# A four-layer graph network on one core: order of TensorE's first work, and transfers of 125 rows issued in two parts

## The chip, the cores and the metric

The kernel runs on one core of a Trainium2 chip. The metric is device time in microseconds (us) of one execution; the median of several runs is quoted, and the profile is of one execution more. The engines are TensorE (PE; its weight loads are shown as PEld), VectorE (DVE), ScalarE (ACT), GpSimd (POOL) and SyncE (SP), which only issues transfers. Each engine runs its own program, and programs meet through semaphores.

## The reference

The input is a graph with N = 1250 nodes of D = 512 features and E = 21250 edges, sorted by receiver `dst` (10000 random pairs in both directions, and 1250 loops). Four layers follow one another, and each is added to its input and normalised over the features:

```python
edge_index = jnp.stack([src, dst])
x = _layernorm(x + L0(x))   # graph attention, 8 heads; batch norm, gelu, plus x @ W_skip + b_skip
x = _layernorm(x + L1(x))   # messages weighted by an MLP of the edges' 8 features, times 4 edge attributes
x = _layernorm(x + L2(x))   # attention over neighbours, then silu(agg) @ base_w.T + cubic splines of agg
x = _layernorm(x + L3(x))   # relu(w @ [x, mean of the neighbours])
```

For L0, with `h = x @ W_gat` in 8 heads, the score of an edge is `leaky(a_src[src] + a_dst[dst])`, a softmax over the edges of each receiver weights `h[src]`, and a sum by receiver follows. L1 gathers `x0, x1 = x @ W_up` at each edge's sender, multiplies by `tpw = MLP(edge_attr_8)` and `edge_attr_4`, and sums by receiver. L2's attention is of the same kind with one head.

## The kernel before, in words

Nodes are cut into NB = 10 blocks of NP = 125 rows, so that most tiles have 125 partitions, and edges into 125 lists of 170.

**First stage.** SP loads dst, src, two tiles of edge attributes and the blocks 5 to 9 of x (L539 to L543), then 16 small attention vectors (L549), clears `recs`, a table of edge records in DRAM (L554), and loads weights. ACT loads the blocks 0 to 4 of x (L1420) and W_gat (L1421). VectorE makes 40 masks of dst and scans them (L1852), whose totals `tot_e` go to TensorE (L814, L815: block totals, "record order"). From their result VectorE (L1866 on) finds each record's position, and POOL scatters the 170 lists of records to `recs` (L717). A second set of masks and a scan (L1908) give totals for the order of the count tiles; TensorE's count_order (L819, L820) answers to them. Then 17 sort rounds follow, each with VectorE (L1949 to L1952), ACT's scale_lanes (L1456) and TensorE's sort_batch (L828).

TensorE's order before is written out by hand: block totals; transposes of x in ten blocks (x_block, L838); gat blocks 0 to 4 (`x @ W_gat`, L845); count_order; w_transposed (transposes of W_gat, L866); attention products (L884); gat blocks 5 to 7; two small products (L891, L892); the sort, with gat blocks 8 and 9 in rounds 3 and 8. ACT copies the results out in the same order (gat_out, L1461).

**The stage's end.** When the scatter is done, ACT loads records back in lanes (L1543) and TensorE transposes them (L1000) for L1's MLP (products to L1025). VectorE's max stage (L2037) and the MLP stand ahead of the attention heads, whose first step is row_products (L1030).

**Later transfers.** L1 stores its blocks `xup` (ACT's copy L1663, SP's store), and POOL gathers from them by edge. L2 makes tiles in VectorE (L2067, L2071) for products with x on TensorE (L1261, L1290); deg, a row sum of all counts, is one reduction (L2314) after the last tile; then the sums are divided (L2319 to L2325), weight_sums (L2331 to L2334, 12 operations) and node_sums (L2344 to L2347) feed the spline products (L1309, L1319). L3 splits `z` in a high and a low part, stores both to `z_rows` (ACT the high parts, SP the low), and POOL gathers some rows of it (big_z, read at L1400 by TensorE). Last, SP stores ten blocks of the output (L672).

Of the kernel before, what the change touches and what calls it, by code (L numbers as in the profile page):

```python
# [7 lines left out]
N, D, E = 1250, 512, 21250  # L8
H, C = 8, 64
# [84 lines left out]
def build(nc, a, out):  # L94
# [8 lines left out]
    with ctx:  # L103
# [328 lines left out]
        s_w0_in = sem("s_w0_in")  # L432
        s_wl2_in = sem("s_wl2_in")
# [97 lines left out]

        def bass_row(v, p):
            return v.rearrange("(a n) -> a n", a=1).to_broadcast([p, v.shape[0]])
# [3 lines left out]
        def _(sp):  # L537

            sp.dma_start(dsti, a["dst"].rearrange("(p e) -> p e", p=NP)).then_inc(s_dst_in, 16)  # L539
            sp.dma_start(srci, a["src"].rearrange("(p e) -> p e", p=NP)).then_inc(s_rec_in, 16)  # L540
            sp.dma_start(a4, a["edge_attr_4"].rearrange("(p e) k -> p e k", p=NP)).then_inc(s_rec_in, 16)
            sp.dma_start(a8, a["edge_attr_8"].rearrange("(p e) k -> p e k", p=NP)).then_inc(s_rec_in, 16)
            sp.dma_start(x_sb[:, HB:, :], a["x"].rearrange("(b p) n -> p b n", p=NP)[:, HB:, :]).then_inc(s_x_in1, 16)  # L543
# [97 lines left out]
            sp.dma_start(cnt_rows.rearrange("(b p) n -> p b n", p=NP), cnt_s[:]).then_inc(s_cntrow_out, 16)  # L641
# [24 lines left out]
            for b in range(NB):  # L666
                sp.wait_ge(s_zlo_ok, b + 1)
                sp.dma_start(z_rows[N + b * NP:N + (b + 1) * NP, :], z_lo[:NP, b, :].bitcast(f32)).then_inc(s_zrow_out, 16)
# [8 lines left out]
        def _(pool):  # L677
# [86 lines left out]
            def gathers(i, par, tiles):  # L764
                pool.wait_ge(s_gld_in0 if par == 0 else s_gld_in1, i * 16 + 16)
                pool.nop(nofuse=True)
                g3 = gld[:, par, :]
                pool.wait_ge(s_sel_ok, i * (2 * TP) + (TP * par + TP))
                pool.nop(nofuse=True)
                pool.tensor_copy(gidx[:, par, :], g3.bitcast(u32).rearrange("p (t k) -> p t k", k=RW)[:, :, R_SRCI])  # L770
                pool.tensor_copy(gslot[:, par, :], g3).then_inc(s_gidx_ok, 1)
                pool.wait_ge(s_gidx_ok, i * 2 + (par + 1))
                if par == 0:
                    pool.wait_ge(s_xup_out0, 16 * NB // 2)
                    pool.wait_ge(s_xup_out1, 16 * NB // 2)
# [16 lines left out]
            pool.wait_ge(s_cntrow_out, 16)  # L792
# [3 lines left out]
            pool.wait_ge(s_zrow_out, 16 * 2 * NB)  # L796
# [6 lines left out]
        def _(pe):  # L803
# [28 lines left out]
            def x_block(b):  # L832
                if b % HB == 0:
                    pe.wait_ge(s_x_in if b == 0 else s_x_in1, 16)
# [582 lines left out]
        def _(act):  # L1417
            A = nc.scalar.activation

            act.dma_start(x_sb[:, 0:HB, :], a["x"].rearrange("(b p) n -> p b n", p=NP)[:, 0:HB, :]).then_inc(s_x_in, 16)  # L1420
            act.dma_start(w_gat, kview(a["L0_gnn_W_gat"])).then_inc(s_w0_in, 16)  # L1421
# [49 lines left out]
            for b in range(HB):  # L1471
                gat_out(b)
            for c in range(KT):
                w_transposed(c)
            act.wait_ge(s_wt_ps, KT + 1)
# [3 lines left out]
            for b in range(HB, NB - 2):  # L1479
                gat_out(b)  # L1480
# [11 lines left out]
            for j in range(ROUNDS):  # L1492
                scale_lanes(j)
                if j in (4, 9):
                    gat_out(NB - 2 + j // 9)
# [163 lines left out]
            def xup_out(b):  # L1659
                act.wait_ge(s_xup_ps, b + 1)  # L1660
                if b >= 2:
                    act.wait_ge(s_xup_out0 if b % 2 == 0 else s_xup_out1, 16 * (b // 2))
# [137 lines left out]
            def store_high(b):  # L1800
                act.wait_ge(s_z_cp, b + 1)
                act.dma_start(z_rows[b * NP:(b + 1) * NP, :], z_hi[:NP, b, :].bitcast(f32)).then_inc(s_zrow_out, 16)
# [32 lines left out]
        def _(dve):  # L1835
# [9 lines left out]
            dve.wait_ge(s_dst_in, 16)  # L1845
# [11 lines left out]
            dve.wait_ge(s_rec_in, 48)  # L1857
# [443 lines left out]
            def half_step(u, hf):  # L2301
# [12 lines left out]
            link(v.tensor_reduce(deg[:], cd, X, ALU.add))  # L2314
# [3 lines left out]
            dve.wait_ge(s_l2_agg, 3)  # L2318
            ins = v.tensor_scalar(rden2, PS[:, 0:3, :].rearrange("p a n -> p (a n)")[:, 0:N], 0.5, None, ALU.max)  # L2319
            ins.then_inc(s_psum_ok, 1)  # L2320
            dve.wait_ge(s_psum_ok, NB)
            link(v.reciprocal(rden2, rden2))
            for f in range(KT - 1):
                dve.wait_ge(s_l2_cp, f + KT)
                v.tensor_tensor(aggT[:, f, :], aggT[:, f, :], rden2, ALU.mult).then_inc(s_aggT_ok, 1)  # L2325
# [9 lines left out]

            def node_sums(g):
# [56 lines left out]
            for g in range(3):  # L2393
                weight_sums(g)
# [130 lines left out]
```

## Time and profile before

| what | us |
|---|---|
| median of 3 runs (lowest, highest) | 1581.47 (1580.15, 1582.06) |
| the profiled execution, its own time | 1582.99 |
| its span in the profile | 1581.48 |
| TensorE busy | 1373.6 (87%) |
| VectorE busy | 1354.2 (86%) |
| ScalarE busy | 903.0 (57%) |
| GpSimd busy | 480.1 (30%) |

The span is the time from the first instruction to the last in the profile; what lies outside it (1.5 us) is start and end. By the page's chain of work that ended last, 51% of the span is TensorE's, 24% VectorE's, 12% issue time, and 5% each ACT's and the transfers'. Rows of a timeline give the start, the duration, the engine and line, output and inputs with shapes, how many, and in brackets how long the engine had been idle and what ended that.

### The profile page before, as it was taken

What the parts mean: (1) busy time and instruction counts of PE and PEld (TensorE: products, weight loads), DVE (VectorE), ACT (ScalarE), POOL (GpSimd) and SP (SyncE); (2) the same over time, 40 slices, a digit from 0 to 9 for tenths busy, and PEclk for the clock granted to TensorE, in tenths of its full rate; (3) what the DMA queues carried; (4) which work ended last, traced back from release to release, by engine and by line L of the source; (5) the groups of instructions that cost most, each with busy time, mean ns of one, the idle gap of its engine ahead of it and who ended that gap; (6) DMA issues with size and microseconds to landing.
All of it is one profiled execution on the core that took longest, in us unless ns stands there. A gap on an engine that the chain in (4) does not pass through costs nothing.

```text
span 1581.5 us, 25111 instructions
## 1 busy us (share of the span) xinstructions
PE 1373.6 (87%) x8237; PEld 885.5 (56%) x8237; DVE 1354.2 (86%) x2065; ACT 903.0 (57%) x1949; POOL 480.1 (30%) x488
## 2 busy tenths in 40 slices
PE   1978898837688887789999999979999999999997
PEld 1555444602333333566666666756667777776465
DVE  8875999899899999759999999777989979996244
ACT  1286555628565565558888888543168849772300
POOL 1788888840000100236666666200000000000000
PEclk9998999859899999689999999989999999999998
DMA  4201000126111210246666766400144444342301
GB/s 128 69 6 9 6 7 7 14 70 192 53 58 48 60 52 17 77 133 212 198 201 193 214 197 196 76 1 1 54 132 135 134 145 170 136 143 69 117 24 43
DMA packets 76686, 150.26 MB, mean 95 GB/s; under 512 B 13722, under 2 KB 32268, under 8 KB 76477
## 3 DMA queue, kind: packets, MB, share of 16 engines
q1 hardware_dynamic: 50531, 83.18, 16.1%
q0 software_dynamic: 23328, 59.50, 15.0%
q10 hardware_dynamic: 2746, 6.59, 1.3%
q8 instruction: 38, 0.62, 0.2%
q14 instruction: 43, 0.35, 0.1%
HBM read 116.13 MB, written 32.91 MB: 94 GB/s over the span
## 4 chain that ended last, share of the span: by engine, by line
PE 51%; DVE 24%; issue 12%; ACT 5%; DMA 5%; DVEq 2%; POOL 0%; SPq 0%; POOLq 0%; ACTq 0%
PE PS L1309 14%; DVE arena L2071 7%; DVE arena L2037 5%; PE PS L1167 5%; PE PS L1261 4%; PE PS L1319 4%; DVE arena L2067 3%; PE PS L931 3%; PE PS L1394 3%; PE PS L1153 3%; DVE arena L2233 3%; ACT arena L1456 2%; PE PS L845 2%; DMA x_sb<-in_x 2%; PE PS L1374 2%
## 5 line engine op out<-in xcount | busy, mean ns | idle before, releaser
L717 POOL DMA_INDIRECT recs<-arena x170 | 239.3, 1408 | 89.4 <-issue 88.8
L1079 PE MATMUL PS<-arena 125*128 125x512 f32 (+1 forms) x480 | 190.1, 533 | 43.4 <-DVE arena L2071 43.3
L781 POOL DMA_INDIRECT arena<-xup,gidx x205 | 194.8, 950 | 104.7 <-issue 52.4
L1167 PEld LDWEIGHTS PS<-arena 128*32 128x32 f32 x3280 | 174.1, 109 | 88.3 <-ACT arena L1694 81.9
L1694 ACT ACTIVATE arena<-arena,gslot 128x32 f32<-128x32 f32 x820 | 186.3, 309 | 55.2 <-PE PS L1167 48.0
L1167 PE MATMUL PS<-arena 128*32 128x128 f32 (+1 forms) x3280 | 201.9, 306 | 6.2 <-DVE arena L2225 3.9
L2225 DVE TENSOR_TENSOR arena<-PS,arena 128x1536 f32<-128x1536 f32 (+1 forms) x103 | 179.0, 1738 | 0.0
L1079 PEld LDWEIGHTS PS<-arena 125*128 125x128 f32 x480 | 85.6, 191 | 147.8 <-issue 77.6
L1626 ACT ACTIVATE arena<-arena,c 125x1250 f32<-125x1250 f32 x80 | 106.7, 1336 | 97.6 <-DVE arena L2067 97.6
L2067 DVE SCALAR_TENSOR_TENSOR arena<-arena,c 125x1250 f32<-125x1250 f32 (+1 forms) x100 | 137.7, 1380 | 14.0 <-ACT arena L1748 12.9
L1309 PE MATMUL PS<-arena,cnt_d 128*125 128x256 f32 x576 | 148.4, 380 | 0.0
L794 POOL DMA_INDIRECT cnt_d<-cnt_rows,bidx_c x1 | 0.9, 946 | 463.8 <-DVE bvalid L2453 463.8
L1309 PE MATMUL PS<-arena 128*125 128x256 f32 x432 | 118.1, 383 | 3.6 <-DVE cnt_d L2347 3.5
L1309 PEld LDWEIGHTS PS<-arena,cnt_d 128*125 128x125 f32 x576 | 108.7, 189 | 16.4
L1153 PE MATMUL PS<-arena 64*128 64x512 f32 x410 | 117.5, 649 | 0.0
L2071 DVE SCALAR_TENSOR_TENSOR arena<-arena,cnt_s 125x1250 f32<-125x1250 f32 x80 | 116.0, 1450 | 0.0
L1512 ACT ACTIVATE arena<-PS 125x626 uint16<-125x626 f32 x102 | 69.2, 692 | 60.1 <-PE PS L931 60.0
L1309 PEld LDWEIGHTS PS<-arena 128*125 128x125 f32 x432 | 81.6, 189 | 30.7 <-issue 20.2
L2221 DVE TENSOR_TENSOR arena<-PS,arena 128x512 f32<-128x512 f32 (+1 forms) x103 | 70.9, 688 | 19.4 <-DMA arena<-xup,gidx 14.8
L931 PE MATMUL PS<-arena 128*125 128x512 bf16 (+1 forms) x408 | 73.1, 311 | 15.8 <-DVE arena L1992 15.4
L2233 DVE TENSOR_TENSOR arena<-PS,arena 128x256 f32 x205 | 84.8, 414 | 1.3 <-PE PS L1167 0.5
L931 PEld LDWEIGHTS PS<-arena 128*125 128x125 bf16 x408 | 44.6, 142 | 63.7 <-DVE arena L1992 38.9
(395 smaller groups left out, 2536.2 us busy)
## 6 DMA issues: line engine op xcount, KB each, us to landing
arena<-in_spline_wT SPq DMA_DIRECT2D x32, 512.0 KB, 4.1
t_rows<-arena SPq DMA_DIRECT2D x18, 512.0 KB, 5.1
arena<-t_rows SPq DMA_DIRECT2D x18, 512.0 KB, 4.5
arena<-uv_rows SPq DMA_DIRECT2D x14, 610.4 KB
arena<-h_rows SPq DMA_DIRECT2D x26, 256.0 KB
h_rows<-arena SPq DMA_DIRECT2D x24, 256.0 KB, 2.8
arena<-xup,gidx POOLq DMA_INDIRECT x205, 3.7
cnt_rows<-cnt_s SPq DMA_DIRECT2D x1, 3051.8 KB
```

The lines of the kernel that those rows point to most:

```text
L717: pool.indirect_dma_start(out=recs, out_offset=bass.IndirectOffsetOnAxis(pos[:, c:c + 1], 0), in_=rec[:, c, :], in_offset=None).then_inc(s ...
L781: pool.indirect_dma_start(out=ring[:, m, :], out_offset=None, in_=xup, in_offset=bass.IndirectOffsetOnAxis(gidx[:, par, m:m + 1], 0))\
L931: ins = t.matmul(PS[:NP, 2 * (n % 3) + q, 0:n1 - n0], oh_dst[:, n % (2 * WP), :, e], oh_src[:, 2 * (n % WP) + e, n0:n1], start=(e == 0), s ...
L1079: ins = t.matmul(PS[:, 3 * par + q, 0:n1 - n0], hs[:, sblk, par * C:par * C + 2 * C], wt[:, sblk % WR, n0:n1], start=(sblk == 0), stop=(sb ...
L1153: t.matmul(PS[:, tpw_bank[(2 * k + q) % 4], :], h3[r, buf, k * 128:(k + 1) * 128], w_m4[r, :], start=True, stop=True, tile_position=(q * H ...
L1167: ins = t.matmul(PS[quad * DB:(quad + 1) * DB, bank, o0 * MUL:o0 * MUL + w], sel4[:, s, v * DB:(v + 1) * DB], prod[:, s, c0 * MUL:c1 * MUL ...
L1309: ins = t.matmul(PS[:NP, bank, c * HD:(c + 1) * HD], lhs, w_part(g, w), start=(s == 0 and m in ((0, 1, 3, 6) if j == 0 else (0, 1, 3))), s ...
L1694: ins = A(sel4[:, s, y * DB:(y + 1) * DB], eq4[:, m // 4, s * DB:(s + 1) * DB], ACT.Copy, scale=gslot[:, par, c + R_Y + y:c + R_Y + y + 1])
L2067: v.scalar_tensor_tensor(dst, U, cc, V, ALU.add, ALU.max).then_inc(ok, 1)
L2071: v.scalar_tensor_tensor(dst, e, 1.0, cm, ALU.min, ALU.mult).then_inc(ok, 1)
L2225: v.tensor_tensor(pr[:, :, :, 1:4, :], w[:, :, :, 1, :].unsqueeze(3).to_broadcast([128, n, 2, 3, MUL]), xg[:, :, 1:4, :].unsqueeze(2).to_b ...
L2233: v.tensor_tensor(d, PS[:, 2 + m % 4, 0:256], d, ALU.add).then_inc(s_gsum_ok, 1)
```

## The change

There are three edits. (1) Every transfer of 125 rows becomes two, one of 112 rows and one of 13, with the counts of the waits doubled: the loads of dst, src, edge attributes and x, the stores of xup, of the count rows, of z (SP's and ACT's) and of the output. (2) TensorE's order in the first stage is x blocks, w_transposed, gat 0 and 1, block totals, attention products, gat 2 to 8, count_order, gat 9, small products, sort (without gat blocks). ACT copies in the same order. W_gat's load has a semaphore of its own. (3) At the spline's start, the reduction for deg is done in two halves, the first ahead of the tiles of half 0 and the second in the old place; the first three weight_sums stand ahead of the wait for TensorE's sums; the products of the aggregate are made in the order 0, 2, 1, and the first silu waits for two of them instead of three.

```diff
+        ROWS = (slice(0, NP // 16 * 16), slice(NP // 16 * 16, NP))
...
-            sp.dma_start(dsti, a["dst"].rearrange("(p e) -> p e", p=NP)).then_inc(s_dst_in, 16)
-            sp.dma_start(srci, a["src"].rearrange("(p e) -> p e", p=NP)).then_inc(s_rec_in, 16)
...
-            sp.dma_start(x_sb[:, HB:, :], a["x"].rearrange("(b p) n -> p b n", p=NP)[:, HB:, :]).then_inc(s_x_in1, 16)
+            for dst_tile, view, done in (
...
+                    (x_sb[:, HB:, :], x_rows[:, HB:, :], s_x_in1)):
+                for r in ROWS:
+                    sp.dma_start(dst_tile[r], view[r]).then_inc(done, 16)
...
-                sp.dma_start(xup[b * NP:(b + 1) * NP, :], xup_st[:, b % 2, :]).then_inc(s_xup_out0 if b % 2 == 0 else s_xup_out1, 16)
+                for r in ROWS:
+                    sp.dma_start(xup[b * NP:(b + 1) * NP, :][r], xup_st[r, b % 2, :])\
+                      .then_inc(s_xup_out0 if b % 2 == 0 else s_xup_out1, 16)
...
-                sp.dma_start(out[b * NP:(b + 1) * NP, :], x_sb[:, b, :]).then_inc(s_out_done, 16)
-            sp.wait_ge(s_out_done, 16 * NB)
+                for r in ROWS:
+                    sp.dma_start(out[b * NP:(b + 1) * NP, :][r], x_sb[r, b, :]).then_inc(s_out_done, 16)
+            sp.wait_ge(s_out_done, 32 * NB)
...
-            pe.wait_ge(s_tot_ok, 1)
-            t.matmul(PS[:NP, 1, 0:NDB], upper[:NP, :NP], tot_e[:], start=True, stop=True)
-            t.matmul(PS[:, 1, 64:64 + NDB], ones[:NP, 0:128], tot_e[:], start=True, stop=True).then_inc(s_order_ps, 1)
+            def record_order():
+                pe.wait_ge(s_tot_ok, 1)
...
             for b in range(NB):
                 x_block(b)
-            pe.wait_ge(s_w0_in, 16 * (1 + 2 * H))
-            for b in range(HB):
-                gat_block(b)
-            count_order()
+            pe.wait_ge(s_wgat_in, 16)
             for c in range(KT):
                 w_transposed(c)
+            for b in range(2):
+                gat_block(b)
+            record_order()
+            pe.wait_ge(s_w0_in, 16 * 2 * H)
             pe.wait_ge(s_wa_cp, KT)
...
-            gat_block(HB)
-            for b in range(HB + 1, NB - 2):
+            for b in range(2, NB - 1):
                 gat_block(b)
+            count_order()
+            gat_block(NB - 1)
...
             for j in range(ROUNDS):
                 sort_batch(j)
-                if j in (3, 8):
-                    gat_block(NB - 2 + j // 8)
...
-                    act.wait_ge(s_aggT_ok, KT + 1 if h else KT - 1 + s)
+                    act.wait_ge(s_aggT_ok, KT + 1 if h else KT if s else KT - 2)
...
+            def degrees(hf):
+                bs = slice(hf * HB, (hf + 1) * HB)
+                link(v.tensor_reduce(deg[:, bs], cd[:, bs, :], X, ALU.add))
+            degrees(0)
             half_tiles(0)
             half_terms(1)
             half_tiles(1)
             for j in range(1, NB):
                 add_tile(j)
-            link(v.tensor_reduce(deg[:], cd, X, ALU.add))
+            degrees(1)
...
+            for g in range(3):
+                weight_sums(g)
+
+            dve.wait_ge(s_l2_agg, 3)
...
+            for f in (0, 2, 1):
+                dve.wait_ge(s_l2_cp, f + KT)
+                v.tensor_tensor(aggT[:, f, :], aggT[:, f, :], rden2, ALU.mult).then_inc(s_aggT_ok, 1)
...
-            for g in range(3):
-                weight_sums(g)
             node_sums(0)
```

## Rows read from the trace of the kernel before

**Rows 1.** Chain of waits: start, duration in us, and what.
```profile
2.60 35.35 DMA x_sb<-in_x
...
689.29 4.10 DMA xup<-arena
...
1159.81 7.97 PE PS L1309 x28
...
1169.49 6.04 PE PS L1309 x28
...
1484.25 14.90 DMA z_rows<-z_lo
...
1504.53 6.21 PE PS L1394 x20
...
1514.41 4.67 PE PS L1394 x20
```

**Rows 2.** Windows: length; busy of five engines; granted clock, DMA share, GB/s.
```profile
8.50:12.50 4.00, 0.00 (x0) 0.00 (x0) 3.97 (x35) 0.08 (x1) 0.00 (x0) 1.00 0.92 246
15.00:20.00 5.00, 0.00 (x0) 0.00 (x0) 5.00 (x1) 0.00 (x0) 0.00 (x0) 1.00 0.32 130
400.00:407.00 7.00, 5.38 (x29) 4.65 (x30) 1.64 (x6) 4.06 (x9) 0.63 (x1) 0.60 0.13 37
658.00:661.00 3.00, 1.97 (x8) 1.45 (x7) 2.85 (x6) 2.98 (x4) 0.00 (x0) 0.50 1.05 373
1450.00:1480.00 30.00, 28.35 (x91) 14.10 (x90) 9.81 (x28) 15.53 (x22) 0.95 (x1) 1.00 0.29 98
1576.00:1580.00 4.00, 0.00 (x0) 0.00 (x0) 0.00 (x0) 0.00 (x0) 0.00 (x0) 0.50 0.31 104
```

**Rows 3.** Timeline of the first stage.
```profile
27.14 0.61 PE L814 MATMUL PS<-tot_e,upper 125*125 125x40 f32 x2 [27.14 <-DVE tot_e L1855]
...
28.97 0.20 DVE L1866 TENSOR_SCALAR ngi_e<-PS 128x40 int32<-128x40 f32 x1
...
38.00 4.64 PE L838 MATMUL PS<-ident,x_sb 125*128 125x125 f32 x20 [5.40 <-DMA x_sb<-in_x]
...
42.43 18.03 PE L845 MATMUL PS<-arena 128*125 128x512 f32 x40
...
45.67 1.38 POOL L717 DMA_INDIRECT recs<-arena  x1 [37.88 <-issue]
...
61.99 1.14 PE L866 MATMUL PS<-ident,arena 128*128 128x128 f32 x8 [0.25 <-ACT arena L1465]
...
63.82 3.75 PE L884 MATMUL PS<-arena 128*128 128x16 f32 x32 [0.69 <-ACT arena L1465]
...
80.18 14.75 ACT L1456 ACTIVATE arena<-arena 125x128 f16<-125x128 f16 x50
...
97.64 0.60 ACT L1461 ACTIVATE arena<-PS 125x512 f32<-125x512 f32 x1 [2.71 <-PE PS L845]
```

**Rows 4.** Timeline of the first stage's end.
```profile
337.88 0.35 ACTq L1543 DMA_DIRECT2D arena<-recs  x1
...
342.60 1.09 PE L1000 MATMUL PS<-ident,arena 128*128 128x128 f32 x4 [24.24 <-DVE mxh L2039]
...
400.72 4.56 PE L1030 MATMUL PS<-ident,uv 125*125 125x125 f32 x20 [8.54 <-DVEq L2057]
```

**Rows 5.** Timeline of the later stages.
```profile
688.67 0.60 ACT L1663 ACTIVATE arena<-PS 125x512 f32<-125x512 f32 x1 [1.91 <-DMA xup<-arena]
...
1062.29 1.65 DVE L2067 SCALAR_TENSOR_TENSOR arena<-arena,c 125x625 f32<-125x625 f32 x2 [2.87 <-ACT arena L1748]
...
1125.11 13.17 DVE L2314 TENSOR_REDUCE deg<-cnt_d 125x10 f32<-125x12500 uint16 x1
...
1159.81 1.88 PE L1309 MATMUL PS<-arena 128*125 128x256 f32 x4 [3.48 <-DVE cnt_d L2347]
...
1504.07 0.47 PE L1400 MATMUL PS<-big_z,big_cnt 128*125 128x512 f32 x1 [2.84 <-ACT big_z L1829]
```

More of the change, by code:

```diff
@@ L537, in _ @@
         def _(sp):
-            sp.dma_start(dsti, a["dst"].rearrange("(p e) -> p e", p=NP)).then_inc(s_dst_in, 16)
-            sp.dma_start(srci, a["src"].rearrange("(p e) -> p e", p=NP)).then_inc(s_rec_in, 16)
-            sp.dma_start(a4, a["edge_attr_4"].rearrange("(p e) k -> p e k", p=NP)).then_inc(s_rec_in, 16)
-            sp.dma_start(a8, a["edge_attr_8"].rearrange("(p e) k -> p e k", p=NP)).then_inc(s_rec_in, 16)
-            sp.dma_start(x_sb[:, HB:, :], a["x"].rearrange("(b p) n -> p b n", p=NP)[:, HB:, :]).then_inc(s_x_in1, 16)
+            x_rows = a["x"].rearrange("(b p) n -> p b n", p=NP)
+            for dst_tile, view, done in (
+                    (dsti, a["dst"].rearrange("(p e) -> p e", p=NP), s_dst_in),
+                    (srci, a["src"].rearrange("(p e) -> p e", p=NP), s_rec_in),
+                    (a4, a["edge_attr_4"].rearrange("(p e) k -> p e k", p=NP), s_rec_in),
+                    (a8, a["edge_attr_8"].rearrange("(p e) k -> p e k", p=NP), s_rec_in),
+                    (x_sb[:, HB:, :], x_rows[:, HB:, :], s_x_in1)):
+                for r in ROWS:
+                    sp.dma_start(dst_tile[r], view[r]).then_inc(done, 16)
             sp.wait_ge(s_wdiag_zero, 1)
@@ L640, in _ @@
             sp.wait_ge(s_psum_ok, NB)
-            sp.dma_start(cnt_rows.rearrange("(b p) n -> p b n", p=NP), cnt_s[:]).then_inc(s_cntrow_out, 16)
+            for r in ROWS:
+                sp.dma_start(cnt_rows.rearrange("(b p) n -> p b n", p=NP)[r], cnt_s[r]).then_inc(s_cntrow_out, 16)
             for g in range(2 * SUBS):
@@ L667, in _ @@
                 sp.wait_ge(s_zlo_ok, b + 1)
-                sp.dma_start(z_rows[N + b * NP:N + (b + 1) * NP, :], z_lo[:NP, b, :].bitcast(f32)).then_inc(s_zrow_out, 16)
+                for r in ROWS:
+                    sp.dma_start(z_rows[N + b * NP:N + (b + 1) * NP, :][r], z_lo[r, b, :].bitcast(f32)).then_inc(s_zrow_out, 16)
             for b in range(NB):
                 sp.wait_ge(s_x_ok, 3 * NB + b + 1)
-                sp.dma_start(out[b * NP:(b + 1) * NP, :], x_sb[:, b, :]).then_inc(s_out_done, 16)
-            sp.wait_ge(s_out_done, 16 * NB)
+                for r in ROWS:
+                    sp.dma_start(out[b * NP:(b + 1) * NP, :][r], x_sb[r, b, :]).then_inc(s_out_done, 16)
+            sp.wait_ge(s_out_done, 32 * NB)
         @block.gpsimd
@@ L811, in _ @@
             pe.wait_ge(s_consts, 1)
-            pe.wait_ge(s_tot_ok, 1)
-            t.matmul(PS[:NP, 1, 0:NDB], upper[:NP, :NP], tot_e[:], start=True, stop=True)
-            t.matmul(PS[:, 1, 64:64 + NDB], ones[:NP, 0:128], tot_e[:], start=True, stop=True).then_inc(s_order_ps, 1)
+            def record_order():
+                pe.wait_ge(s_tot_ok, 1)
+                t.matmul(PS[:NP, 1, 0:NDB], upper[:NP, :NP], tot_e[:], start=True, stop=True)
+                t.matmul(PS[:, 1, 64:64 + NDB], ones[:NP, 0:128], tot_e[:], start=True, stop=True).then_inc(s_order_ps, 1)
             def count_order():
@@ L1418, in _ @@
             A = nc.scalar.activation
-            act.dma_start(x_sb[:, 0:HB, :], a["x"].rearrange("(b p) n -> p b n", p=NP)[:, 0:HB, :]).then_inc(s_x_in, 16)
-            act.dma_start(w_gat, kview(a["L0_gnn_W_gat"])).then_inc(s_w0_in, 16)
+            for r in ROWS:
+                act.dma_start(x_sb[r, 0:HB, :], a["x"].rearrange("(b p) n -> p b n", p=NP)[r, 0:HB, :]).then_inc(s_x_in, 16)
+            act.dma_start(w_gat, kview(a["L0_gnn_W_gat"])).then_inc(s_wgat_in, 16)
             def ln_sqrt(layer, b):
@@ L1470, in _ @@
                   PS[:, 4 + b % 2, :].rearrange("p (k n) -> p k n", k=KT)[:, :, 0:NP], ACT.Copy).then_inc(s_xt_cp, 1)
-            for b in range(HB):
-                gat_out(b)
             for c in range(KT):
                 w_transposed(c)
+            for b in range(2):
+                gat_out(b)
             act.wait_ge(s_wt_ps, KT + 1)
@@ L1477, in _ @@
             A(wa[:, :, 0:2 * H], PS[:, 2, 0:KT * 2 * H].rearrange("p (k n) -> p k n", k=KT), ACT.Copy).then_inc(s_wa_cp, 1)
-            for b in range(HB, NB - 2):
+            for b in range(2, NB):
                 gat_out(b)
@@ L1801, in store_high @@
                 act.wait_ge(s_z_cp, b + 1)
-                act.dma_start(z_rows[b * NP:(b + 1) * NP, :], z_hi[:NP, b, :].bitcast(f32)).then_inc(s_zrow_out, 16)
+                for r in ROWS:
+                    act.dma_start(z_rows[b * NP:(b + 1) * NP, :][r], z_hi[r, b, :].bitcast(f32)).then_inc(s_zrow_out, 16)
             def x3_in(b):
@@ L2313, in _ @@
                 add_tile(j)
-            link(v.tensor_reduce(deg[:], cd, X, ALU.add))
+            degrees(1)
             link(v.tensor_scalar(cen[:], cen[:], -KAPPA, KAPPA * (1.0 + 1.0 / STEP), ALU.mult, ALU.add))
[L2318 to L2325, printed above, removed]
             def weight_sums(g):
@@ L2334, in weight_sums @@
                 v.tensor_tensor(t4, b21, t2w, ALU.subtract)
+            for g in range(3):
+                weight_sums(g)
+            dve.wait_ge(s_l2_agg, 3)
+            ins = v.tensor_scalar(rden2, PS[:, 0:3, :].rearrange("p a n -> p (a n)")[:, 0:N], 0.5, None, ALU.max)
+            ins.then_inc(s_psum_ok, 1)
+            dve.wait_ge(s_psum_ok, NB)
+            link(v.reciprocal(rden2, rden2))
+            for f in (0, 2, 1):
+                dve.wait_ge(s_l2_cp, f + KT)
+                v.tensor_tensor(aggT[:, f, :], aggT[:, f, :], rden2, ALU.mult).then_inc(s_aggT_ok, 1)
             def node_sums(g):
```

19 lines of the change are left out of this document (9 added, 10 removed).

## The prediction

> **What bounds the kernel now.** I read the chain of waits first: it names the work that ended last, and an edit off it gains nothing by itself. Seven of its rows carry this forecast [rows 1]. It begins with one transfer, the second half of x, from 2.60 for 35.35 us, and goes on in TensorE's work on x. Later it runs through the stores of blocks and their read-back: 4.10 us for an xup store, 14.90 us for the last z store.
>
> The windows by stretch say why these are long [rows 2]. While only transfers of 125 rows run (15 to 20, and 1576 to 1580) the DMA share is 0.32 and 0.31, at 130 and 104 GB/s: five engines in sixteen are at work. From 8.5 to 12.5, where W_gat (128 rows) runs beside x, the share is 0.92 at 246 GB/s; with 128-row loads alone, from 658, it is 1.05 at 373 GB/s.
>
> Third I read the timelines. In the first stage [rows 3] TensorE waits at L814 for the totals (27.14) and at L838 for x's second half (38.00). At the stage's end [rows 4] the attention heads start at 400.72, behind 8.54 us of waiting on VectorE's max stage. The MLP ahead of them started only at 342.60, when the scattered records came back from the load at 337.88. So two chains lead to the heads: the sort and max stage on VectorE, and scatter, record load and MLP.
>
> **Term 1, first stage: −6.0 us.** The start loads 2 × 1.28 MB of x, 1.05 MB of W_gat, 0.085 MB each of dst and src and 1.02 MB of edge attributes: 4.8 MB. With all parts on sixteen engines at the 373 GB/s of the 128-row row, that is 12.9 us; from a first byte at about 2.0 and with 1.3 us to land, the second half of x is there at about 16.3 (22.8 at the 246 GB/s of the mixed row) instead of 37.95. Both rates are bounds from rows; parts of 112 and 13 rows appear in neither, and I take the faster, since its transfers are alone, as these would be.
>
> TensorE then does its blocks 5 to 9 (4.64 us, L838), w_transposed (two groups like L866's, 2.5 us with the wait between; up to 3.9 cold) and two gat blocks. L845's five blocks took 18.03, so 3.6 us each; I allow 7.8 for two, with a cold start. The new wait for W_gat stands ahead of all this; its load is shared out with x's and should be in by 16 too, and while it isn't, everything on TensorE is held. The block totals, which before ran at 27.14, come at 16.3 + 4.6 + 3.9 + 7.8 = 32.6 and end at 33.1. VectorE's next step, L1866, goes from 28.97 to 33.2: **4.2 us late**. This is the cost of the new order: totals wait behind work that is not urgent. The 4.2 us goes rigidly into the record positions and POOL's scatter (first at 45.67), which is 170 issues long and doesn't depend on the sort. The records' load thus comes at 342.1 instead of 337.88. Before, L1000 began 4.7 us after that issue and last waited for VectorE's mxh, so the load was in earlier, by something between 0 and 2 us; with 0.7 the MLP is 3.5 us late.
>
> SP's queue: the attention loads (L549), the clearing of recs and the loads after them stand behind x's second half and come about 20 us earlier; the products (L884, 3.75 us) wait for them at 33.2, behind the totals, and they should be in by some 27. If they weren't, gat blocks 2 to 8 and count_order would wait too. The count order itself comes at 33.1 + 3.75 + 7 × 3.6 + 0.5 = 62.6, against 42.43 + 18.03 = 60.5 before: 2 us later, with 19.7 us between it and the sort's start on ACT at 80.18.
>
> The sort gains. Its start at 80.18 follows gat_out of block 7, and inside it two gat blocks cost ACT 2.71 us of waiting and 0.60 of work each [rows 3]: 2 × 3.31 = 6.6 us. Blocks 8 and 9 now lie before it; TensorE is through with block 9 by 67, so that the start, which followed block 7 at 80, is VectorE's to set and may move up by 1 or 2. So 6.6 to 8.6; I take 8.3, and VectorE reaches the heads at 392.3. The MLP is the later one: its last product before the heads came 8.54 us ahead of 400.72, at 392.2, plus 3.5 = 395.7. The heads gain 400.7 − 395.7 = 5.0.
>
> The clock: from 400 to 407 the granted clock is 0.60, after TensorE has idled through those 8.54 us, and L1030's 20 transposes take 4.56 us. With no idle ahead of them at full clock they would take as little as half; between 0 and 2.3 I take 1.0. Sum: −6.0.
>
> **Term 2, xup stores: −3.3.** Two stores follow one another on the chain, the last 4.10 us; ACT's L1663 waits 1.91 us for the first of the two [rows 5]. A store is 256 KB, so 2.3 us at some 111 GB/s (the rows give 98 to 130 [rows 2]) and 1.75 us of fixed time. At 373 GB/s the bytes take 0.7: −1.6 and −1.7. Lower bound nothing, if the second part's issue (about 0.3 us on SP) and landing cost what the bytes save.
>
> **Term 3, spline start: −1.6.** The degree reduction L2314 is 13.17 us, after VectorE's last tile [rows 5]. Half of it, 6.6, now stands before the tiles, where VectorE had 2.87 us of idle (L2067 at 1062.29). The other 3.7 to 3.8 us delays the tiles and the aggregation behind them. TensorE ends that at 1156.3 + 3.8 = 1160.1 and finds its input made, where before it idled 3.48 us (L1309): VectorE has saved the other half of the reduction, and the weight sums no longer stand in line. So +3.8 − 3.48. The first spline group behind the idle took 7.97 us, the next 6.04 [rows 1]; without the idle, −1.93. Together −1.6. Bounds: +0.3 if the clock gives nothing back and −5.4 if the added half hides entirely.
>
> **Term 4, z rows: −4.4.** The last z store takes 14.90 us, its bytes queued behind nineteen others on five engines; its gather ends near 1503.3, and TensorE has waited 2.84 us at L1400 (1504.07) [rows 5]. With sixteen engines the queue is empty as the last store is issued (some 4 us for it), and big_z is there at about 1492, nine us before TensorE can use it. The wait goes: −2.84. The two groups behind it took 6.21 and 4.67 [rows 1]; the excess of 1.54 goes if TensorE doesn't slow for the pause. Bounds −2.8 and −4.4; I take −4.4, as the pause is gone wholly. ACT's extra issues for the high parts sit in its idle time.
>
> **Term 5, the end: −3.5.** The last two output blocks are 512 KB. At 104 GB/s that is 4.9 us, at 373 1.4: −3.5; at 246 GB/s −2.8, and with the second part's issue inside it −2.
>
> **What is costed at nothing.** cnt_rows' store in two parts: its reader comes 300 us later. Loads of src and edge attributes: VectorE finds them in already. The order f 0, 2, 1 in the aggregate products lets the first silu start sooner; it is part of finding the input made.
>
> Sum −6.0 − 3.3 − 1.6 − 4.4 − 3.5 = −18.8. The profiled execution took 1582.99 us (span 1581.48): 1564.2. The median of the runs, 1581.47, is 1.5 below it: **1562.7**.
>
> **A rule that speaks against it.** The Trainium skill, DMA: Bandwidth & Descriptors, section Rules for kernel authors, says of two transfers to disjoint partition halves not to bother, as both spread over all 16 engines anyway, and to use one 128-partition transfer. By that rule every DMA term would be nothing (rival 4). The share of 0.32 says the premise is not met here: 125 rows are on five engines. The same page, section Why a DMA increments its semaphore by 16 and not by 1, says that the number of engines is the largest up to 16 that divides the slowest dimension: 125 gives 5, as the rows show, 112 gives 16 and 13 gives 13, which no run here shows yet.
>
> **Rivals.**
> 1. *Loads at the mixed rate.* The second half of x lands at 22.8, and L1866 is 10.7 us late; the MLP is ready 10.0 late at 402.2. Term 1 is +1.5 instead of −6.0, and term 5 −2.8: sum −10.6, **1570.9**. For it: 246 GB/s was measured with x in the mix. Against: the mix there was limited by x's five engines.
> 2. *The scatter is not the limit.* If the totals come earlier (a warm TensorE, W_gat in time) or the scatter absorbs the delay, VectorE's chain decides, term 1 is −8.3: **1560.4**. For it: the scatter's only row is its first issue, and its pace is not read here. Against: 170 issues in a row, with the record load at the end of them, leave nothing to catch up with.
> 3. *Stores gain nothing* because landing, not bytes, is what they cost. Terms 2 and 5 are 0, and term 4 −2.8: sum −10.4, **1571.1**. Against: three rows at 98 to 130 GB/s, so that bytes are more than half of a store.
> 4. *The other side: the two parts run no faster than one transfer.* The second half of x still lands at 37.95, and the totals stand behind it: 37.95 + 4.6 + 3.9 + 7.8 + 0.5 = 54.8 instead of 28; L1866 is 26 late, the MLP 25 late, ready at 417.5: +16.8. Terms 2, 4, 5 are 0, with −1.6: +15.2, **1596.7**. It decides once x lands later than about 35. For it is only that no row shows such parts; against, the 0.32.
>
> **How the numbers follow.** My case 0.52, rival 1 0.18, rival 2 0.12, rival 3 0.12, rival 4 0.06. The range runs from rival 2 with term 3 at its low bound (1560.4 − 3.8) to just above rivals 1 and 3: **1556.5 to 1572**. With each case's own spread that leaves out rival 4 and about one in ten of the others. A change under 0.2% (3.2 us) is about what a measurement can't tell from none; only a landing of x between those of rivals 1 and 4 gives that, 0.03, taken from rivals 1 and 3. Faster 0.91, same 0.03, slower 0.06.
>
> **What would show it.** In the changed trace: DMA share near 0.9 from 3 to 15, and x's second half landed by 17; L1866 near 33; first scatter near 50; no ACT wait for gat inside the sort; heads near 395 with TensorE waiting on the MLP; xup stores near 2.4 us; no idle before L1309 at the spline's start; no wait at L1400; under 2 us from the last store's issue to its data. The prediction is wrong above all if a part of 13 rows is as slow as the whole, or if the order of TensorE's first work matters more than 4.2 us.

## The result, and the profile after

The changed kernel took 1584.66 us (median of 12 runs, 1578.32 to 1591.73) beside 1580.0 for the kernel before (12 runs, 1575.91 to 1582.35). The medians differ by 4.7 us; the ratio is 1.0035 (interval 1.002 to 1.0049), so about 5.5 us slower where 18.8 us faster was forecast. The profiled execution took 1584.27 us with a span of 1582.70, 1.2 us more than before's span. The profiled execution of before (1582.99) lies above all 12 of that kernel's runs, which is why the profiles differ by less than the medians; the rows below account for the 1.2 us.

Setting the two traces side by side shows where the time went and where it came back. Each row is the same event in both; the last column is what the stretch since the row above cost.

| event | before | after | later by | stretch |
|---|---|---|---|---|
| first scatter issue (L717, now L729) | 45.67 | 54.55 | 8.9 | +8.9 |
| record load on ACT (L1543, now L1555) | 337.88 | 362.85 | 25.0 | +16.1 |
| attention heads on TensorE (L1030, now L1043) | 400.72 | 416.53 | 15.8 | −9.2 |
| last but one xup store | 684.58 | 697.85 | 13.3 | −2.5 |
| VectorE's first product with xup (L2221, now L2234) | 699.89 | 709.25 | 9.4 | −3.9 |
| second spline group (L1309, now L1322) | 1169.49 | 1176.80 | 7.3 | −2.1 |
| second z group (L1394, now L1407) | 1514.41 | 1518.81 | 4.4 | −2.9 |
| end of the span | 1581.48 | 1582.70 | 1.2 | −3.2 |

From the heads on, 14.6 us are won, near the 13.8 of the forecast (terms 2 to 5 and the clock). All of the loss, and more, is in the first stage. These are the rows of the changed kernel's timeline there (start, duration, what, idle before and its end), which answer to [rows 3] and [rows 4].

```profile
23.67 4.51 PE L851 MATMUL PS<-ident,x_sb 125*128 125x125 f32 x20 [8.85 <-DMA x_sb<-in_x]
...
27.64 0.23 DVE L1868 TENSOR_TENSOR tot_e<-cnt_d 125x39 f32<-125x39 f16 x1
...
37.19 0.31 PE L827 MATMUL PS<-tot_e,upper 125*125 125x40 f32 x2
...
37.84 0.20 DVE L1879 TENSOR_SCALAR ngi_e<-PS 128x40 int32<-128x40 f32 x1 [8.02 <-PE PS L828]
...
54.55 1.38 POOL L729 DMA_INDIRECT recs<-arena  x1 [46.80 <-issue]
...
115.03 15.44 POOL L729 DMA_INDIRECT recs<-arena  x1 [0.30 <-issue]
...
342.07 2.46 POOL L729 DMA_INDIRECT recs<-arena  x1 [0.30 <-issue]
...
358.98 2.45 POOL L729 DMA_INDIRECT recs<-arena  x1 [0.31 <-issue]
...
362.85 0.36 ACTq L1555 DMA_DIRECT2D arena<-recs  x1
...
367.87 1.09 PE L1013 MATMUL PS<-ident,arena 128*128 128x128 f32 x4 [53.63 <-DMA arena<-recs]
...
416.53 2.45 PE L1043 MATMUL PS<-ident,uv 125*125 125x125 f32 x20
```

Three things are to be seen. x's second half lets TensorE go on at 23.67, 14 us earlier than before, but not at 16.3. The totals are ready on VectorE at 27.9 and wait until 37.19 for TensorE, and VectorE stands idle for 8.02 us. And the scatter, once started, takes longer: one issue holds POOL for 15.44 us, and six of the last ones take 2.46 where before they took 1.17. The groups of instructions by line say the same in one row each, the kernel before first (busy us, mean ns of one, idle before):

```profile
L717 POOL DMA_INDIRECT recs<-arena x170 | 239.3, 1408 | 89.4 <-issue 88.8
```

```profile
L729 POOL DMA_INDIRECT recs<-arena x170 | 255.4, 1502 | 98.3 <-issue 98.3
```

8.9 us later to begin and 16.1 us longer: that is the 25.0. What VectorE does beside the long issue stands in the windows from 100 to 130.5, for before and then for the changed kernel (columns as in [rows 2]):

```profile
115.00:130.50 15.50, 10.81 (x110) 9.15 (x112) 13.46 (x16) 14.92 (x51) 13.06 (x9) 1.00 0.08 6
```

```profile
100.00:115.00 15.00, 8.38 (x85) 7.55 (x86) 14.58 (x23) 12.56 (x42) 12.52 (x8) 1.00 0.09 7
115.00:130.50 15.50, 11.85 (x122) 8.99 (x119) 14.83 (x19) 14.97 (x51) 15.44 (x1) 1.00 0.02 2
```

Before, VectorE is busy 13.46 of 15.5 us and POOL works on nine issues. In the changed kernel VectorE is busy 14.83 and POOL works on one.

The busy time alone doesn't decide it. From 78.3 to 90.9 the changed kernel's VectorE goes through five rounds of the same three instructions without any gap, and POOL works on eight issues, none above 1.82 us:

```profile
78.30:90.90 12.60, 7.75 (x62) 6.83 (x63) 12.60 (x15) 12.13 (x42) 10.47 (x8) 0.70 0.10 8
```

### The profile page after: what moved, and what is told of

It reads as the page before. It is cut to its first block, busy times and chain, and to the rows that moved or that the text cites. A ratio compares the mean times of both kernels' runs of the same rounds, so it can differ in the third digit from the quotient of the medians.

```text
span 1582.7 us, 25159 instructions
## 1 busy us (share of the span) xinstructions
PE 1362.1 (86%) x8237; PEld 875.6 (55%) x8237; DVE 1351.7 (85%) x2066; ACT 903.7 (57%) x1949; POOL 496.0 (31%) x488
## 3 DMA queue, kind: packets, MB, share of 16 engines
q1 hardware_dynamic: 51395, 83.19, 16.3%
## 4 chain that ended last, share of the span: by engine, by line
PE 38%; issue 19%; DVE 19%; POOL 16%; DVEq 3%; DMA 2%; ACT 2%; SPq 0%; POOLq 0%; ACTq 0%
POOL recs L729 15%; PE PS L1322 14%; DVE arena L2084 7%; DVE arena L2246 4%; PE PS L1274 4%; PE PS L1332 4%; DVE arena L2080 3%; PE PS L1407 3%; PE PS L1387 2%; PE PS L1397 2%; DVEq L2246 2%; PE PS L1303 1%; DMA x_sb<-in_x 1%; PE PS L1231 1%; DVEq L2257 1%
## 5 line engine op out<-in xcount | busy, mean ns | idle before, releaser
L729 POOL DMA_INDIRECT recs<-arena x170 | 255.4, 1502 | 98.3 <-issue 98.3
L1322 PE MATMUL PS<-arena,cnt_d 128*125 128x256 f32 x576 | 147.8, 379 | 0.0
L1322 PEld LDWEIGHTS PS<-arena,cnt_d 128*125 128x125 f32 x576 | 108.1, 188 | 16.2
L1322 PE MATMUL PS<-arena 128*125 128x256 f32 x432 | 116.8, 379 | 0.1
L1322 PEld LDWEIGHTS PS<-arena 128*125 128x125 f32 x432 | 81.0, 188 | 26.6 <-issue 16.4
L944 PE MATMUL PS<-arena 128*125 128x512 bf16 (+1 forms) x408 | 73.7, 313 | 16.2 <-DVE arena L2005 15.8
L2234 DVE TENSOR_TENSOR arena<-PS,arena 128x512 f32<-128x512 f32 (+1 forms) x103 | 71.0, 689 | 16.6 <-PE PS L1166 13.9
```

The lines of the kernel that those rows point to most:

```text
L729: pool.indirect_dma_start(out=recs, out_offset=bass.IndirectOffsetOnAxis(pos[:, c:c + 1], 0), in_=rec[:, c, :], in_offset=None).then_inc(s ...
L944: ins = t.matmul(PS[:NP, 2 * (n % 3) + q, 0:n1 - n0], oh_dst[:, n % (2 * WP), :, e], oh_src[:, 2 * (n % WP) + e, n0:n1], start=(e == 0), s ...
L1322: ins = t.matmul(PS[:NP, bank, c * HD:(c + 1) * HD], lhs, w_part(g, w), start=(s == 0 and m in ((0, 1, 3, 6) if j == 0 else (0, 1, 3))), s ...
```

## The experiments

Theory A is what the rows suggest: the loss sits in the scatter, which starts late because the totals stand behind work that isn't urgent, and which stalls where VectorE works without gaps. The rivals: B, the transfers in two parts slow what shares their queues; C, the order has no part in it. What was measured is given as the ratio to the kernel before, with its interval.

**The two suspects, one at a time and together.** First the totals moved up behind the x blocks:

```diff
             for b in range(NB):
                 x_block(b)
+            record_order()
             pe.wait_ge(s_wgat_in, 16)
...
             for b in range(2):
                 gat_block(b)
-            record_order()
```

> The changed kernel with the block totals moved up, right behind the ten x blocks and ahead of w_transposed and the two gat blocks. Theory A (the loss sits in the scatter: it starts 8.9 us late behind TensorE's unhurried work, and is stretched by some 16 us where VectorE's sort rounds leave it no gap): the totals run at about 28.2 instead of 37.2, the first scatter at about 45.5 instead of 54.6, but one scatter issue of some 15 us stays; the record load starts at about 353 instead of 362.9, the heads 9 to 14 us earlier, the whole 0.992 to 0.997 of before. Theory B (the parts of 112 and 13 rows slow everything that shares their queues): the scatter is as long as in the changed kernel whatever starts it, and the whole gains 9 at most. Theory C (the order has no part in it): no change against the changed kernel, 1.0035 of before.

Measured: 0.994 (0.9921 to 0.9959). Theory C falls. The first issue is at 46.70 and the record load at 345.41, better than expected; the long issue is still there.

```profile
116.70 15.43 POOL L729 DMA_INDIRECT recs<-arena  x1 [0.30 <-issue]
...
342.47 1.53 POOL L729 DMA_INDIRECT recs<-arena  x1 [0.30 <-issue]
...
345.41 0.36 ACTq L1555 DMA_DIRECT2D arena<-recs  x1
...
399.68 2.45 PE L1043 MATMUL PS<-ident,uv 125*125 125x125 f32 x20 [1.38 <-DVEq L2070]
```

Busy time of the scatter: 245.8, so the gapless sort alone costs it 6.5 us (the long issue holds work that would elsewhere have been stretched a little, too). TensorE's heads now wait for VectorE again, if only for 1.38.

Second, gat blocks 8 and 9 back in the sort, with ACT's copies of them, the totals left late:

```diff
-            for b in range(2, NB - 1):
+            for b in range(2, NB - 2):
                 gat_block(b)
             count_order()
-            gat_block(NB - 1)
...
                 sort_batch(j)
+                if j in (3, 8):
+                    gat_block(NB - 2 + j // 8)
```

> The changed kernel with gat blocks 8 and 9 back in sort rounds 3 and 8, as in the kernel before; the totals stay late. Theory A: with TensorE's gat blocks in them the sort rounds leave VectorE waiting now and then, the scatter issue of 15.4 us is gone (none above 4 us between 100 and 140), the scatter ends 8 to 16 us earlier than in the changed kernel, its start stays at 54.6; the whole 0.992 to 0.998 of before. Theory B: the scatter's busy time stays near 255 us. Theory C (a longer sort only costs): 3 to 6 us slower than the changed kernel, since VectorE's chain to the heads gets longer.

Measured: 0.9927 (0.9912 to 0.9943). The scatter starts at 54.18, its busy time is 240.6 and the record load comes at 347.71, 15.1 us earlier. One issue of 5.03 us remains at 113.68, above the 4 expected, and two of 2.46 at the end.

Third, both edits:

> Both: totals right behind the x blocks, and gat blocks 8 and 9 back in the sort. Theory A: first scatter near 45.5, busy time of the scatter near 240 as before, record load near 338, heads at about 400 as before or some us earlier, and all the later gains (13 us) stay: 1562 to 1569, 0.988 to 0.993 of before. Theory B: the scatter stays near 255 us and the whole no better than 0.995.

Measured: 0.9912 (0.9898 to 0.9926), 1565.71 us. Busy 236.5, record load at 336.39, and TensorE waits 8.22 us for VectorE ahead of the heads (397.53), as before the change.

So the 16.1 us of stretching divide like this. Late but not gapless: +1.3. Gapless but on time: +6.5. Both at once: +16.1, and the 8.3 left over belong to the two together. Most of them are at the scatter's end: six issues of 2.46 us there cost 6 × (2.46 − 1.2) = 7.6, where the gapless version that starts on time has none and the late one with gat blocks in the sort has two. VectorE's max stage, whose rows of the changed kernel follow, shows what runs beside them.

```profile
337.56 1.45 DVE L2050 CUSTOM_DVE_ANT_0 arena<-arena,PS 125x1250 bf16<-125x1250 bf16 x1
339.26 1.46 DVE L2050 CUSTOM_DVE_ANT_0 arena<-arena 125x1250 bf16<-125x1250 bf16 x1
340.65 1.45 DVE L2050 CUSTOM_DVE_ANT_0 arena<-arena 125x1250 bf16<-125x1250 bf16 x1
342.03 1.46 DVE L2050 CUSTOM_DVE_ANT_0 arena<-arena 125x1250 bf16<-125x1250 bf16 x1
```

Until 339 one operand comes from PSUM (PS), and scatter issues beside it take 1.17; from 339.26, with the later heads, both come from SBUF. Of the nine issues from there on six take 2.46 and start every 2.76 us, two instructions of VectorE's; the others take 1.50 (the first) and 1.17 and 1.31 (around a change of head at 353). Before, that part began at 342.53, and the scatter was through at 336.5. A scatter that comes late is made later still. That the operands' place is the reason is read from rows side by side; no run varied it alone.

**Only the gaps.** To separate the gaps from the gat blocks, the changed kernel with one wait made stricter:

```diff
-                if j >= SBUFS:
-                    dve.wait_ge(s_order_ps, 3 + j - SBUFS)
+                if j >= 2:
+                    dve.wait_ge(s_order_ps, 3 + j - 2)
```

> The changed kernel with one wait made stricter: in the sort VectorE starts round j when TensorE has done round j−2, not j−3, so that it can no longer run three rounds ahead and then work without a gap. The totals stay late, and no gat block is moved. Theory A (the scatter stalls while VectorE works without a gap): the issue of 15.4 us falls apart into ones below 4 us, the record load comes 6 to 14 us earlier than the changed kernel's 362.9 with the scatter's start unchanged at 54.6, the sort is 1 to 3 us longer; the whole 0.992 to 0.998 of before. Theory B' (it was the gat blocks' place that mattered, by TensorE's timing or the clock): the long issue stays and the time is that of the changed kernel, 1.002 to 1.005, or slower for the wait.

Measured: 0.9915 (0.9894 to 0.9935), 1566.93 us, a little better than expected: the change's loss turned into a gain by making VectorE wait. The window of the sort's second half, and the longest issue in it:

```profile
115.00:130.50 15.50, 10.08 (x105) 8.45 (x105) 13.98 (x22) 14.93 (x50) 13.16 (x8) 1.00 0.08 7
```

```profile
118.03 3.23 POOL L729 DMA_INDIRECT recs<-arena  x1 [0.30 <-issue]
```

POOL works on eight issues again, with VectorE busy 13.98 of 15.5. Record load 349.72 (−13.1). Theory B' is out: no gat block was moved. The cost to the sort was missed: its last round starts at 133.51 instead of 126.74, 6.8 us later where 1 to 3 were expected.

**Totals first, and the stricter wait** (both edits shown above):

> The changed kernel with the totals right behind the x blocks and the stricter wait in the sort, gat blocks all ahead of the sort. Theory A: scatter from about 46.8, busy about 237 to 240, record load at 336 to 340; the sort without gat blocks ends 2 to 4 us earlier than with them, so the heads come at 398 to 402 (VectorE's max stage is the limit); 0.988 to 0.992 of before, the best so far or equal to it. If the long issue of 15 us stays, record load near 345 and 0.994 as with the totals moved alone.

Measured: 0.9899 (0.9884 to 0.9914), 1565.33 us, the lowest ratio of all, though its interval overlaps with that of both edits above (0.9912). Record load 336.52; the heads at 399.13 wait 8.63 us for VectorE. The sort is not shorter for having no gat blocks in it: its last round starts at 131.71, with them at 125.97.

**What ends a hold, and what starts one.** In every trace but that of the stricter wait alone, an issue that starts 2.23 to 2.25 us after VectorE's four additions in the sort's eleventh round (L1974) is held, and wherever the trace lists VectorE's next wait, the issue ends 1.05 or 1.06 us after that wait begins. The rows of the issue and of the end of that wait: the kernel before, gat blocks in the sort, and totals first with the stricter wait.

```profile
115.90 2.43 POOL L717 DMA_INDIRECT recs<-arena  x1 [0.30 <-issue]
...
117.42 0.83 DVE L1949 TENSOR_TENSOR arena<-iota,arena 125x1280 f16<-125x1280 f16 x1 [0.15 <-PE PS L828]
```

```profile
113.68 5.03 POOL L729 DMA_INDIRECT recs<-arena  x1 [0.30 <-issue]
...
118.55 0.82 DVE L1965 TENSOR_TENSOR arena<-iota,arena 125x1280 f16<-125x1280 f16 x1 [0.89 <-PE PS L841]
```

```profile
117.05 2.42 POOL L729 DMA_INDIRECT recs<-arena  x1 [0.30 <-issue]
...
118.61 0.82 DVE L1962 TENSOR_TENSOR arena<-iota,arena 125x1280 f16<-125x1280 f16 x1 [0.20 <-PE PS L841]
```

In the changed kernel, and with the totals alone moved, no such wait comes, and the issue ends 1.05 us after the last round's last product (129.42 and 131.08). So in each of these runs the hold lasts until VectorE waits or the rounds are over. What starts one stays open: the five gapless rounds from 78.3 hold nothing for long, and with the stricter wait alone the issue of 3.23 us, which starts 1.44 us after the additions, ends while VectorE works on without a gap. That run by itself therefore doesn't show whether the waits or the issue's shifted start spared it the long hold; the one with the totals first does, where the issue starts at the usual place and ends with a wait of 0.20 us.

**The change's parts alone.** First all transfers in two parts in the kernel before, with its orders: of the change's diff only the lines with ROWS and the doubled counts, and W_gat on its old semaphore:

```diff
+            act.dma_start(w_gat, kview(a["L0_gnn_W_gat"])).then_inc(s_w0_in, 16)
```

> The kernel before with the transfers in two parts and nothing else: TensorE's and ACT's order and the spline's start as before. Theory A: x's second half lands near 23.6 and the totals run at about 28; scatter as before (start near 46, busy near 240); sort up to 5 us earlier; later terms from xup, z rows and the end some 11 us: 0.990 to 0.995 of before. Theory B: scatter busy near 255, record load 10 us or more later than before, the whole no better than before. A rule against splitting transfers would have it at 1.000.

Measured: 0.9955 (0.994 to 0.997), just outside what was expected, which its interval reaches. The scatter is as before (first issue 46.33, busy 237.8, record load 337.06): theory B falls.

Then only the stores (xup, count rows, z, output), each as here, with the counts of their waits:

```diff
-                sp.dma_start(out[b * NP:(b + 1) * NP, :], x_sb[:, b, :]).then_inc(s_out_done, 16)
+                for r in ROWS:
+                    sp.dma_start(out[b * NP:(b + 1) * NP, :][r], x_sb[r, b, :]).then_inc(s_out_done, 16)
```

> The kernel before with only the stores in two parts (xup, count rows, z rows, output); loads, orders and spline start as before. The forecast's terms 2, 4 and 5 came to 3.3 + 4.4 + 3.5 = 11.2; the profile of the changed kernel gives some 5.2 + 2.9 + 3.2 = 11.3 for the same places. Theory: 9 to 12 us faster, 0.992 to 0.995. Theory of the rule against splitting: 1.000. If the gains at these places come in part from elsewhere (clock, other loads), 4 to 8 us.

Measured: 0.9929 (0.9917 to 0.9942), 11 us. And only the loads (dst, src, edge attributes, x):

```diff
+                for r in ROWS:
+                    sp.dma_start(dst_tile[r], view[r]).then_inc(done, 16)
```

> The kernel before with only the loads of the start in two parts. The forecast held x's landing to be what sets the first stage. Theory A: x's second half lands 14 us earlier (23.6 for 37.95), but the totals wait for VectorE's scan, which starts 0.9 us later as dst now lands at 7.8 among the others, so the heads and the end come 0 to 2 us later: 1.000 to 1.0015. If x's landing counted: 3 to 6 us faster.

Measured: 1.0005 (0.9994 to 1.0016), nothing. dst lands later among the other loads: VectorE begins at 8.01 and not at 5.45, and the totals are done at 28.06 and not at 27.0. TensorE's 5.40 us of waiting for x are gone, but nothing is won by it: TensorE now waits 4.37 us for VectorE's totals of the count order, its attention products take 7.01 us instead of 3.75, and it reaches the sort's small products at 81.36 instead of 79.58. Why the products take longer was not tested. Stores alone gain 11 us, loads alone nothing, and yet all transfers together only 0.9955, about 4 us less than the stores alone, with intervals that just touch; that was not explained.

Only the spline's start, the change's lines from `degrees` on with the silu's wait:

```diff
+            degrees(0)
             half_tiles(0)
...
-            link(v.tensor_reduce(deg[:], cd, X, ALU.add))
+            degrees(1)
```

> The kernel before with only the spline's start changed (deg in two halves, weight sums moved up, order 0, 2, 1). The forecast's term 3 is −1.6; between the same places the changed kernel's profile gives about −2. Theory: 1 to 3 us faster, 0.998 to 0.9995, so within 0.2%. If the degrees' first half simply adds its 6.7 us ahead of the tiles: 2 to 4 us slower.

Measured: 0.9993 (0.998 to 1.0006), so no gain that can be told from none. And the stores' lines together with the spline's:

> The kernel before with the stores in two parts and the spline's start changed; loads in one part and the first stage's order as before. Theory A: it has all that the change gives and nothing of what it costs: 0.990 to 0.992 of before, equal to or 1 to 2 us better than the two repaired versions with the new order. If the loads or the new order are worth something in the repaired versions: 0.993 to 0.995.

Measured: 0.9921 (0.9905 to 0.9937). Its interval overlaps with those of the two repaired versions, so whether the new order, repaired, is worth 0 to 3 us stays open.

**The rate of the start's loads.** On the version with both repairs (totals first, gat blocks in the sort), SP issued ACT's loads, too:

```diff
-            for r in ROWS:
-                act.dma_start(x_sb[r, 0:HB, :], a["x"].rearrange("(b p) n -> p b n", p=NP)[r, 0:HB, :]).then_inc(s_x_in, 16)
-            act.dma_start(w_gat, kview(a["L0_gnn_W_gat"])).then_inc(s_wgat_in, 16)
+                    (x_sb[:, 0:HB, :], x_rows[:, 0:HB, :], s_x_in),
...
+            sp.dma_start(w_gat, kview(a["L0_gnn_W_gat"])).then_inc(s_wgat_in, 16)
```

> The version with the totals first and gat blocks in the sort, with x's first half and W_gat issued by SP behind the edge attributes instead of by ACT: all loads of the start in one queue. It tests why the start moved about 250 GB/s at a DMA share of 1.05, where 128-row loads from 658 moved 373. Theory P (two queues with interleaved transfers cost the difference): over 350 GB/s from 6 to 14, x's second half in by 15 to 17 instead of 23.6. Theory Q (that is the rate of these loads, whichever queue): 240 to 270 GB/s, and x's second half in by 19 to 21, since W_gat now stands behind it, the first half later than 10.6. In both the heads don't move by more than 1 us, since the scan, not x, sets the totals: 0.989 to 0.993.

Measured: 0.9902 (0.9888 to 0.9916), as without this edit. The windows of its start:

```profile
4.00:8.00 4.00, 0.00 (x0) 0.00 (x0) 3.93 (x6) 0.00 (x0) 3.78 (x7) 1.00 0.91 276
8.00:12.00 4.00, 0.00 (x0) 0.00 (x0) 4.00 (x37) 0.00 (x0) 0.00 (x0) 1.00 1.04 254
12.00:16.00 4.00, 0.39 (x2) 0.42 (x3) 3.97 (x4) 0.00 (x0) 0.00 (x0) 1.00 1.08 228
```

It is theory Q in the main: 252 GB/s from 4 to 16 at a full share with one queue, 256 from 3 to 15 in the changed kernel with two. x's second half lets TensorE go on at 21.77, a little later than the 19 to 21 expected. Why these loads move less than the 373 of the later ones [rows 2] was not found.

## Why the prediction was wrong, step by step

**Term 1, first stage: forecast −5.0 at TensorE's heads (and −1.0 by the clock), measured +15.8 there.** This is the step that failed, and in it one sentence: the 4.2 us "goes rigidly into the record positions and POOL's scatter", which "is 170 issues long and doesn't depend on the sort". The scatter was taken as 170 issues of fixed length, and its pace was not read. It isn't fixed, and it does depend on the sort: its busy time is 255.4 us instead of 239.3. The record load comes 25.0 us late instead of 4.2, 8.9 of it by the late start and 16.1 by the stretching, and the MLP's slack of 8.5 is overrun. An issue that is held goes through when VectorE waits. The gain of the sort was booked without asking what VectorE's waits were good for: taking TensorE's gat blocks out of the rounds took away VectorE's waits for TensorE (0.15 to 1.19 us a round from 117 on in the kernel before), and these were what ended the hold there after 2.43 us.

The Trainium skill, SBUF — State Buffer, section SBUF: two separate sides, warns of this kind of thing: VectorE and GpSimd share a port pair as an exclusive lock, which a VectorE instruction holds for its whole length in certain modes, in which GpSimd can't write the descriptors of the transfers that it issues, or with two SBUF inputs beside a GpSimd instruction that reads SBUF. The runs agree in part: the sort's three instructions have two SBUF inputs, the scatter's offsets lie in SBUF, and an issue of 1.17 us undisturbed is held for 15.44 beside them, and in the max stage issues take mostly 2.46 where both inputs are in SBUF and 1.17 where one is in PSUM. The lock itself is in no trace, and a lock of one instruction's length explains neither a hold across some twenty nor the gapless rounds from 78.3, which let issues through.

Also in term 1:
- The landing of x's second half was forecast at 16.3 and came at 23.6. Rival 1 had it at 22.8, from the mixed row's 246 GB/s; the changed kernel moved 258 at a share of 1.07 from 8.5 to 12.5. Preferring 373 was the wrong choice between two rows: at a share of 0.92, the mixed row had all but shown the full-share rate. It cost 7.3 us; TensorE's work between x and the totals gave 2.7 of them back (9.0 us from 28.2 to 37.2, where 3.9 + 7.8 was allowed), so the totals were 8.9 late instead of 4.2.
- The sort was to bring VectorE to the heads 8.3 us earlier. It came 3.3 us earlier (397.35 for 400.6, where its idle before the heads begins), and that is what the sort gave: its rounds end at 129.4 instead of 132.8. The 8.3 was read from ACT's waits. VectorE's own waits for TensorE in the sort of before, 8.8 us with 6.05 after the third round, are all gone, but its first round starts at 77.92 instead of 71.84: VectorE comes to the count order 8.9 us later, with the late totals, and waits there 1.82 us more for TensorE, which makes it at 66.94 where 62.6 was forecast.
- The slack of the MLP chain was read rightly (8.5 us). The gapless sort alone leaves 1.38 us of it, the late totals alone nothing (heads at 401.23 for 400.72), and both versions are still faster than before. Both together overrun it by 16 us.
- L1043's transposes took 2.45 for 4.56, −2.1 (forecast −1.0), since TensorE no longer idles ahead of them (granted clock 0.99 from 416 to 424, where it was 0.60 from 400 to 407).

**Term 2, xup stores: forecast −3.3, measured −3.9.** The two stores on the chain of waits after the change:

```profile
697.50 0.30 SPq L627
697.85 2.36 DMA xup<-arena
...
700.92 0.30 SPq L627
701.26 1.96 DMA xup<-arena
```

They were 4.00 and 4.10 [rows 1]. Ahead of each now stands the issue of the first part, so the two gain some 3.1 us on the chain.

**Term 3, spline: forecast −1.6, measured −2.1** between the same places in the traces, and 0.9993 alone, which the timed runs can't tell from nothing. The first half of deg takes 6.67 us ahead of the tiles, TensorE goes from the aggregation to the spline products without a pause, and the two groups are alike:

```profile
1069.57 6.67 DVE deg L2324
...
1169.04 6.04 PE PS L1322 x28
...
1176.80 6.04 PE PS L1322 x28
```

**Term 4, z rows: forecast −4.4, measured −2.9.** The wait at L1400 is gone and the groups take 4.65 and 4.67, so what was forecast came. But in the same stage a group of products behind an idle of 1.65 us now takes 5.39 where it took 3.70; the granted clock from 1455 to 1475 is 0.92, and was 1.00 from 1450 to 1470. What made the clock fall behind the same idle was not tested. The row of before, and those of the changed kernel:

```profile
1464.14 3.70 PE L1374 MATMUL PS<-arena 128*125 128x512 f32 x8 [1.65 <-DVE z_lo L2464]
```

```profile
1471.45 5.39 PE L1387 MATMUL PS<-arena 128*125 128x512 f32 x8 [1.65 <-DVE z_lo L2482]
...
1502.17 4.62 PE PS L1407 x20
...
1510.49 4.65 PE PS L1407 x20
```

**Term 5, the end: forecast −3.5, measured −3.2.** From 1580 to 1581 the stores move 254 GB/s at a share of 0.85 (before 104 at 0.31 [rows 2]).

Terms 2 to 5 were forecast at −12.8 and came to −12.1; alone, stores and spline give −12.5 in the timed runs (0.9921). **Rival 4**, the one on the other side, had the right place (the totals behind other work, the MLP late) and a wrong cause: the parts do run on all engines. That its +16.8 for the heads is near the measured +15.8 is luck. The rule against splitting that spoke for it is refuted for 125 rows: 11 us for the stores, which also ends **rival 3**. **Rival 2** supposed the scatter not to be the limit, and said of its pace that it was not read; that question, asked of the rows, would have found lengths from 1.17 to 6.90 us, the longest beside VectorE's second scan (L1908).

The version with the totals first and the stricter wait takes 1565.33 us. By its ratio it is 16 us faster than the kernel before, where 18.8 was forecast for the changed kernel.

## What to carry to other kernels

Before a wait is taken out of one engine's program, look for who lives on the gap: here a held transfer of POOL's went through in VectorE's waits, and a denser sort cost more than it won. A chain of many small issues has no fixed length; read its longest issues and what runs beside them, as well as its mean. And when a small, urgent step is moved behind large ones, ask what its result starts: the block totals are about 1 us of TensorE's work and start 290 us of scatter.

## What the runs showed of the hardware

- An indirect transfer's issue on POOL took 1.17 us beside a VectorE instruction that reads PSUM, mostly 2.46 beside the same one with both operands in SBUF, and 15.44 across some twenty VectorE instructions without a gap. The issue held in the sort ended 1.05 us after VectorE's next wait began. Other gapless stretches of the same instructions let issues through in 1.18 to 1.57 us; what starts a hold is not known.
- Parts of 112 and 13 rows of a 125-row transfer fill the engines (share 0.85 to 1.07 instead of 0.31), and a 256 KB store takes 2.3 to 2.7 us, the first part's issue included, instead of 4.0 to 4.1.
- The loads of the start moved about 250 GB/s at a full share; the changed kernel's from 25 to 28 moved 360, and those from 658 in the kernel before 373. One queue or two made no difference at the start.
